# Tokens placed in PSUM by identity products ahead of the aligned sums

## The reference, cut to what matters

```python
def _align_one(small, large):                 # small = context, large = tokens
    D = _pairwise_euclidean(small, large)
    R = _dtw_cost(D)                          # forward pass over the rows of R
    i_idx, j_idx, valid = _backtrack(R, T_small, T_large)
    contrib = small[i_idx] * valid[:, None].astype(small.dtype)
    return jnp.zeros((T_large, d), dtype=small.dtype).at[j_idx].add(contrib)
...
def _L0_ffn_ref(x, w1, b1, w2, b2):
    h = quantized_relu(quantized_linear(x, w1, b1))
    return quantized_linear(h, w2, b2)
...
x = x + _L0_xattn_ref(ctx_1024, _layernorm(x, axis=-1))
x = x + _L0_ffn_ref(_layernorm(x, axis=-1), L0_ffn_w1, L0_ffn_b1, L0_ffn_w2, L0_ffn_b2)
```

## Time and profile before

| what | value |
|---|---|
| median of 3 runs | 191.33 us |
| lowest and highest run | 191.01 and 192.35 us |
| the profiled execution's own time | 191.8 us |
| span of the profiled execution, from first to last instruction | 189.9 us |
| instructions | 3733 |
| busy: PE, PEld, DVE, ACT, POOL | 101.5, 68.4, 154.4, 101.8, 37.6 us |

### The profile page before, as it was taken

The page is one execution under the profiler, slowest core; times in us unless marked ns, Lnnn a source line. Parts: engine busy times, 40 slices in busy tenths (PEclk is TensorE's granted clock), DMA queues, the critical chain, the costliest instruction groups (busy, mean ns, idle before and its releaser), DMA issues.

```text
span 189.9 us, 3733 instructions
## 1 busy us (share of the span) xinstructions
PE 101.5 (53%) x1239; PEld 68.4 (36%) x1239; DVE 154.4 (81%) x754; ACT 101.8 (54%) x183; POOL 37.6 (20%) x97
## 2 busy tenths in 40 slices
PE   0789951000270000000001977978999999998991
PEld 0779850000140000000000333644666666665671
DVE  1994866999999999999998089797989989996351
ACT  3776766299991000044050009677686867777720
POOL 8964463000000000000000000002222405132250
PEclk9999997555555555555555599999999999999998
DMA  5993004800079500020112420004417354472847
GB/s 180 349 348 122 7 5 140 332 0 0 5 250 337 187 0 0 0 71 0 69 69 76 61 34 11 3 0 55 51 13 105 42 74 58 54 79 40 105 56 168
DMA packets 19603, 16.89 MB, mean 89 GB/s; under 512 B 5760, under 2 KB 19200, under 8 KB 19456
## 3 DMA queue, kind: packets, MB, share of 16 engines
q1 hardware_dynamic: 14336, 12.69, 20.7%
q0 software_dynamic: 3808, 3.67, 15.9%
q10 hardware_dynamic: 1440, 0.30, 0.8%
HBM read 7.48 MB, written 9.18 MB: 88 GB/s over the span
## 4 chain that ended last, share of the span: by engine, by line
DVE 46%; PE 40%; ACT 4%; issue 4%; DMA 3%; DVEq 0%; SPq 0%
PE y L1225 12%; PE h L1208 6%; DVE Y L1008 6%; DVE R L801 5%; PE t L1208 3%; DVE A L769 3%; DVE enter L995 3%; DVE bcarry L994 3%; PE e L1169 3%; DVE carry L789 3%; DVE M L790 3%; PE h L1121 3%; DMA X<-in_x_dram 3%; PE y L1238 2%; PE t L1121 2%
## 5 line engine op out<-in xcount | busy, mean ns | idle before, releaser
L466 POOL DMA_DIRECT2D out_dram<-E x14 | 17.0, 1217 | 137.2 <-DVE E L980 137.2
L1225 PE MATMUL y<-w2T,XT 128*128 128x256 bf16 x256 | 37.7, 273 | 0.4 <-DVE XT L970 0.4
L1238 PE MATMUL y<-w1T 128*128 128x512 bf16 x19 | 6.7, 513 | 46.6 <-DVE S_lo L1022 46.6
L1225 PEld LDWEIGHTS y<-w2T,XT 128*128 128x128 bf16 x256 | 25.0, 98 | 14.7 <-DVE XT L970 0.7
L616 ACT ACTIVATE h_int<-h,b_s 128x512 int16<-128x512 f32 x37 | 25.4, 686 | 5.6 <-PE h L1208 5.0
L1208 PE MATMUL h<-M,w1T 128*128 128x512 bf16 x74 | 21.9, 380 | 1.7 <-ACT M L609 1.6
L1238 PEld LDWEIGHTS y<-w1T 128*128 128x128 bf16 x19 | 2.1, 123 | 50.1 <-DVE S_lo L1022 46.9
L622 ACT ACTIVATE code<-Y,shifts 128x640 bf16<-128x640 bf16 x3 | 2.5, 828 | 32.5 <-DVE enter L995 32.5
L970 DVE TENSOR_SCALAR XT<-h_int 128x1024 bf16<-128x1024 int16 x28 | 12.1, 439 | 9.0 <-ACT h_int L616 9.0
L1158 PE MATMUL t<-ident_bf,w_raw 128*128 128x128 bf16 x32 | 4.6, 312 | 22.6 <-ACT w_raw L561 21.0
L616 ACT ACTIVATE h_int<-t,b_s 128x512 int16<-128x512 f32 x19 | 13.0, 686 | 3.1 <-PE t L1208 2.9
(11 more groups left out here) (195 smaller groups left out, 266.5 us busy)
## 6 DMA issues: line engine op xcount, KB each, us to landing
X<-in_x_dram SPq DMA_DIRECT2D x8, 512.0 KB, 8.2
out_dram<-b_s SPq DMA_DIRECT2D x7, 512.0 KB, 5.5
out_dram<-E POOLq DMA_DIRECT2D x14, 256.0 KB, 4.3
w_raw<-in_L_ffn_w_dram SPq DMA_DIRECT2D x2, 1024.0 KB, 5.9
S<-in_ctx_dram SPq DMA_DIRECT2D x1, 512.0 KB, 3.8
out_dram<-E SPq DMA_DIRECT2D x4, 128.0 KB, 2.7
path_dram<-A SPq DMA_DIRECT2D x3, 160.0 KB, 1.8
path_dram<-XT SPq DMA_DIRECT2D x3, 160.0 KB, 1.9
```

The costliest lines, as they stand in the source:

```text
L466: nc.gpsimd.dma_start(tiles_out[:, b:b + 2, quad_of(g), :], res[:, g % 2, 2 * h:2 * h + 2, :], accum_op=ALU.add).then_inc(out_stored[g % 2 ...
L1225: mm = nc.tensor.matmul(bank67[t // 2][:, t % 2, :], hq[:, g % 2, n, t * P:t * P + P], w2T[:, n, :], start=(n == 0 and not bias), stop=(n ...
L1238: nc.tensor.matmul(bank67[0][:, :, :].rearrange("p j d -> p (j d)"), w1T[:, 0, 0:P], w1T[:, 0, 0:512], start=True, stop=True)
```

## The change

Identity products (`ident` stationary, `X` moving, both fp32) write the tokens of groups 0 and 1 into PSUM, and the aligned products of these groups accumulate on them there. For this group 0 gets `bank23` and `bank67`, group 1 gets `bank01[0]` and `bank5`, and the warm-up products write to `bank01[1]`. DVE no longer adds for these groups. For group 0 it takes its statistics directly from PSUM, and then ACT copies the sums to `X` (`copy_sums`, one for each half); for group 1 ACT copies first (`copy_next`, two 128x512 copies), and DVE takes the statistics from `X`. The second `keep_warm` has 5 products in place of 7 and stands behind the four `align`. `align(2, 0)` waits for group 0's copies. DVE does all four clips of the first half behind `spread_of(1)`. `tokens_T(1)` moves from behind the half steps to behind n = 6 of the second half, ahead of `hidden_half(1, 7)`.

```diff
-WARM = (10, 7, 2)
+WARM = (10, 5, 2)
...
+        early_bank = [bank01[0], bank5]
+
+        def early_sum(g, j, h):
+            return (bank23, bank67)[j][h][:, 0, :] if g == 0 else early_bank[h][:, D * j:D * j + D]
...
+            def copy_sums(j):
+                act.wait_ge(sums_read, 2 * j + 2)
+                for h in range(2):
+                    nc.scalar.activation(X[:, 2 * j + h, :], early_sum(0, j, h), ACT.Copy).then_inc(sums_copied[0], 1)
+
+            def copy_next():
+                act.wait_ge(aligned, 4)
+                for h in range(2):
+                    nc.scalar.activation(X[:, 4 + h:8:2, :], early_bank[h][:, :].rearrange("p (j d) -> p j d", j=2),
+                                         ACT.Copy).then_inc(sums_copied[1], 1)
...
             act.wait_ge(b_clip, 2)
+            copy_sums(0)
             deviation_half(0)
+            copy_next()
             copy_half(0)
+            copy_sums(1)
             deviation_half(1)
...
             def spread_half(j):
+                v.wait_ge(aligned, j + 1)
                 for h in range(2):
-                    v.wait_ge(x1_ready, 2 * j + h + 1)
-                    nc.vector.bn_stats(stats2[:, 2 * j + h, :], X[:, 2 * j + h, :]).then_inc(dve_order, 1)
-                own[0] += 2
-                v.wait_ge(dve_order, own[0])
+                    nc.vector.bn_stats(stats2[:, 2 * j + h, :], early_sum(0, j, h)).then_inc(sums_read, 1)
+                v.wait_ge(sums_read, 2 * j + 2)
...
             def quantise_half(j):
                 v.wait_ge(std2_ready, j + 1)
+                v.wait_ge(sums_copied[0], 2 * j + 2)
...
             def spread_of(g):
 
                 for h in range(2):
-                    v.wait_ge(x1_ready, 2 * g + h + 3)
+                    if g == 1:
+                        v.wait_ge(sums_copied[1], h + 1)
+                    else:
+                        v.wait_ge(x1_ready, 2 * (g - 2) + h + 1)
...
-            add_half(0)
             spread_half(0)
-            add_half(1)
             quantise_half(0)
             spread_half(1)
-            add_row(1, 0)
             quantise_half(1)
-            add_row(1, 1)
-            clip_half(0, 0)
-            clip_half(0, 1)
             spread_of(1)
-            clip_half(0, 2)
-            clip_half(0, 3)
+            for m in range(NH // 2):
+                clip_half(0, m)
             quantise(1)
...
+            def place_tokens(g):
+                for t in range(4):
+                    if g == 0:
+                        nc.tensor.matmul(early_sum(g, t // 2, t % 2), ident[:, :], X[:, t, :], start=True, stop=False)
+                    elif t < 2:
+                        nc.tensor.matmul(early_bank[t][:, :], ident[:, :], X[:, 4 + t:8:2, :], start=True, stop=False)
...
             def align(g, j):
 
                 pe.wait_ge(path_in[g // 2], 16 * 8)
-                if g >= 1 and j == 0:
-                    pe.wait_ge(x1_ready, 2 * g + 2)
+                if g == 2 and j == 0:
+                    pe.wait_ge(tokens_quantised, 2)
+                    pe.wait_ge(sums_copied[0], 2)
+                if g >= 3 and j == 0:
+                    pe.wait_ge(x1_ready, 2 * (g - 2))
+                early = g < 2
                 for part, third in enumerate((S_hi, S_mid, S_lo)):
                     for h in range(2):
                         at = I * h
-                        mm = nc.tensor.matmul(bank23[h][:, j, :], PB[at:at + I, g, 2 * j + h, :],
-                                              third[at:at + I, batch_of(g, 2 * j) // 2, :], start=(part == 0), stop=(part == 2))
+                        sums = early_sum(g, j, h) if early else bank23[h][:, j, :]
+                        mm = nc.tensor.matmul(sums, PB[at:at + I, g, 2 * j + h, :],
+                                              third[at:at + I, batch_of(g, 2 * j) // 2, :], start=(part == 0 and not early),
+                                              stop=(part == 2 and (g != 1 or j == 1)))
                 mm.then_inc(aligned, 1)
...
                 if n == 0:
                     pe.wait_ge(xqT_copied, j + 1)
+                    pe.wait_ge(sums_copied[1], 2)
...
             def output(g, part):
 
                 t, n0 = part // 2, (part % 2) * (NH // 2)
+                if part == 0 and g == 0:
+                    pe.wait_ge(sums_copied[0], 4)
...
             pe.wait_ge(pool_const, 16)
             pe.wait_ge(b_clip, 2)
             pe.wait_ge(wT_copied, NH)
+            pe.wait_ge(prods_made, 4 * LOADS)
+            pe.wait_ge(std_ready, LOADS)
+            pe.wait_ge(sum_copied, LOADS)
+            for g in range(2):
+                place_tokens(g)
 
...
-                    nc.tensor.matmul(bank67[0][:, :, :].rearrange("p j d -> p (j d)"), w1T[:, 0, 0:P], w1T[:, 0, 0:512],
+                    nc.tensor.matmul(bank01[1][:, :], w1T[:, 0, 0:P], w1T[:, 0, 0:512],
                                      start=True, stop=True)
 
             keep_warm(WARM[0])
-            align(0, 0)
-            align(0, 1)
+            for g in range(2):
+                for j in range(2):
+                    align(g, j)
             keep_warm(WARM[1])
-            align(1, 0)
-            align(1, 1)
             tokens_T_half(0)
             keep_warm(WARM[2])
...
                 if n in (5, 7):
                     align(2, n // 2 - 2)
-            tokens_T(1)
+                if n == 6:
+                    tokens_T(1)
```

More of the change, by code:

```diff
@@ L247, in align_ffn_kernel @@
         x1_ready = sem("x1_ready")
+        sums_read = sem("sums_read")
+        sums_copied = [sem(f"sums_copied{g}") for g in range(2)]
         var2_ready = sem("var2_ready")
@@ L893, in add_row, with spread_half @@
                 nc.vector.tensor_tensor(xv, bank23[h][:, :, :], xv, ALU.add).then_inc(x1_ready, 1)
-            def add_half(j):
+            def spread_half(j):
+                v.wait_ge(aligned, j + 1)
                 for h in range(2):
[L897 to L901, removed]
-                    v.wait_ge(x1_ready, 2 * j + h + 1)
-                    nc.vector.bn_stats(stats2[:, 2 * j + h, :], X[:, 2 * j + h, :]).then_inc(dve_order, 1)
-                own[0] += 2
-                v.wait_ge(dve_order, own[0])
+                    nc.vector.bn_stats(stats2[:, 2 * j + h, :], early_sum(0, j, h)).then_inc(sums_read, 1)
+                v.wait_ge(sums_read, 2 * j + 2)
                 for t in range(2 * j, 2 * j + 2):
```

## The result

The changed kernel takes 195.27 us by the median of 4 runs (194.81 to 195.43); the kernel before took 191.84 us by 4 runs on the same chip (191.01 to 192.81). The ratio is 1.0168, with a 95% interval from 1.013 to 1.0207: slower, by 1.7%, about 3.2 us. The forecast was 195.2 us, which was 191.33 us and 3.9 us on top. The profiled execution has a span of 193.6 us and took 195.42 us.

A forecast was written before the change was run, and what follows sets the result against it. PE is full from hidden(2, 0), so a delay reaching its start passes on whole. Terms 4.1 - 1.5 + 0.5 + 0.8 = +3.9 us on 191.33 gave 195.2 us; 8-in-10 range 193.4 to 196.6 us.

The forecast's parts named there:

- Part 1: PE's list: identity products stay behind the wait for S_lo, starting at 103.79 us, not in PE's idle time.
- Part 2: Identity products on PE: 2048 columns at 4 cycles each, 8192 cycles, 3.41 us at 2.4 GHz.
- Part 3: PE's clock rises at 109.6 us, 5.8 us after PE begins; first align starts 4.1 us later.
- Part 4: First align to first turn of group 0: 3.8 us in place of 5.29, a gain of 1.5 us.
- Part 5: ACT ahead of the first rounding: group 1's copies before the root make that rounding 0.5 us later than PE's product.
- Part 6: `tokens_T(1)` ahead of hidden_half(1, 7) waits for `quantise(1)` and delays `align(2, 1)` and DVE's add of group 2: +0.8 us.
- (a): Rival: identity products do run in PE's idle time during the passes; +0.2 us, 191.5 us; chance 0.04.
- (b): Rival: identity products on PE cost 2 cycles a column, like transposes; +2.2 us, 193.5 us; chance 0.10.
- (d): Rival: PE's clock rises only 5.8 us after warm-up begins, or falls before group 0; +7 us, 198.4 us; chance 0.06.
- (c): Rival: front as forecast, but Part 6 or Part 5 costs nothing, since DVE runs ahead; +3.1 us, 194.4 us; chance 0.25.

The follow-up runs named there:

- e1: Changed kernel with the wait for S_lo moved from ahead of the identity products to between them and the first warm-up; 191.31 us, 0.9972 of the kernel before.
- e4: Changed kernel with every identity product issued twice, the first time as a closed group; 198.14 us, 1.0337 of the kernel before.
- e2: e1's kernel with the turn of group 1 (`tokens_T(1)`) put back behind the half steps; 190.82 us, 0.9954 of the kernel before.
- e3: Changed kernel with only the turn of group 1 (`tokens_T(1)`) put back behind the half steps; 194.78 us, 1.0159 of the kernel before.
- e5: Changed kernel without its ten first warm-up products; 193.51 us, 1.005 of the kernel before.
- e7: Kernel before, with 28 warm-up products from row 3 of the backward pass in place of ten behind S_lo; 192.13 us, ratio 1.001.
- e6: Changed kernel with identity products and 26 warm-up products from row 10 of the backward pass, `tokens_T(1)` put back; 189.50 us, 0.9857 of the kernel before.
- e8: Kernel before, with 36 warm-up products from row 10 of the backward pass in place of ten behind S_lo; 190.25 us, ratio 0.9912.
- e9: e6's kernel with 22 warm-up products in place of 26; 189.60 us, 0.9884 of the kernel before.

## Why the prediction was right

**Part 1** (the wait for S_lo stays ahead of the products) is what decided, and it held: 104.10 us, released by S_lo. e1, which moves only that wait, takes 4 us away.

**Part 2**, 4 cycles a column, held (e4: 4.03). The Trainium skill, "FP8 and Floating Point Precision", TensorE Precision Notes, gives four passes through the array for true fp32. e4's 4.03 cycles a column agree with it; the trace itself has two records for each product, of 2 cycles a column each.

**Part 3**, +4.1 us to the first align, was +4.43 us from S_lo's end. About half of the difference is the clock, which rose 6.1 us after the first product (at 110.2 us) where I had put 5.8 us. The other half is the first group of products: the next one starts 1.87 us behind it, where the others are 1.70 us apart.

**Part 4**, a gain of 1.5 us, was 1.79 us. ACT's two copies take 0.66 us together and hold back the root by 0.55 us, and not 0.9; the two statistics take 0.85 us up to the copies, and not 0.75.

**Part 5**, +0.5 us on ACT ahead of the first rounding, was mis-sized: turn 0 moved by 2.96 us and the first rounding by 2.99 us, so the term measured 0.03 us. The second pair of copies starts at 117.35 us and the root at 117.88 us, while the first hidden product (117.51 us) is still under way, and the rounding follows that product by 0.46 us where it was 0.43 us.

**Part 6**, +0.8 us, was 0.95 us at add 2 (3.94 less 2.99), and e2 and e3 give the move 0.87 us by itself.

The sum from S_lo's end is 4.43 - 1.79 + 0.03 + 0.95 = 3.62 us; S_lo itself ended 0.32 us later in this trace, and add 2 and hidden(2, 0) stand 3.94 us later. The span grew by 3.7 us, 0.2 us less.

The path and its waits were right; that the number fits to 0.1 us is partly luck, in two ways. Parts 3 and 6 came out larger than I had put them, parts 4 and 5 smaller in cost, and these errors nearly cancelled. And the forecast stood on 191.33 us, the median of three runs, while the kernel before had 191.84 us with a fourth: by the medians the change costs 3.4 us and by the ratio 3.2 us (interval 2.5 to 4.0 us), not 3.9.

Of the rivals, (a) is what e1 made true. Its number, 191.5 us, is near e1's 191.31, but it had the kernel 0.2 us slower, and e1 is 0.3% faster (interval 0 to 0.6%). (b) is refuted by e4, where a column costs 4 cycles, and (d) by the changed kernel itself, where the clock is up at 110.2 us while identity products run. (c) was right in one half: part 5 did cost nothing, and part 6 did cost. Its +3.1 us is as near to the measured 3.2 us as the forecast is, so the time does not tell them apart; the rows of parts 5 and 6 do. One reading of the rows was loose: DVE is not full from the start, its busy tenths are 4 to 8 in several of the first seven slices. Nothing in the sum rests on it.

## What to carry to other kernels

Work that is meant for an idle stretch is only there if every wait ahead of it in its engine's list is over by then; find the first row of the new work in the trace and read what released it before arguing about its price. Products that serve as warm-up should start by an event of the stage before and be as many as the input's arrival allows: tied to the last event of that stage they are on the path (e5), and too many of them hold the input up (e7). When the first stages of a program vary by a microsecond from run to run, read each trace from the event at which the kernels begin to differ.

## What the runs showed that I had not expected

- The time from the first product of a dense row to the rise of the clock was not steady. It was 5.8 us in the kernel before, 6.1 us in the changed one, 5.3 us in e5, 5.2 us in e3, 4.8 us in e1 and e6, 4.7 us in e8, 4.3 us in e4, 3.0 us in e9, 2.6 us in e2 and 2.5 us in e7 (101.64 to about 104.1 us). Two kernels that are equal up to turn 0 differ there by 0.45 us (the changed one and e3) and 0.99 us (e1 and e2), nearly all of it from this, and a fixed count of warm-up products is sometimes too many.
- Executions of one kernel differ by 0.8 us with their mean granted clock (e7's numbers above), and a profile shows one of them. Where in the run the lower mean comes from is not shown: the clock also falls at different times after the first stage, at 30.9 us in e1 and 33.4 us in e4.
- In e1 the clock rose at 61.6 us, under identity products, which ended at 63.7 us; PE was idle then, and the clock was down again at 68.4 us. Products placed that early warm nothing up for the third stage.
- bn_stats of a 128x256 fp32 tile costs the same from PSUM (0.76 us for two) as from SBUF (0.74 us for two).
- ACT's copy of 128x256 fp32 from PSUM to SBUF takes 0.66 us for two in a row.
- PE's products beside DVE's passes slowed these by nothing that stands out: S_lo ended at 104.26 to 104.75 us in e6 to e9, and at 103.73 to 105.03 us in the kernels without such products.
- In the first stage the page gives a granted clock of 0.9 and more while eight transposes took 1.94 us against 1.04 us later: that is half the pace, so there the pace of the products tells the clock, and the page's row does not.
